# Two-head row maxima on two 64-row tiles of TensorE instead of four 32-column tiles

## The chip, the cores and the metric

The kernel runs on one core of a Trainium2 chip. The metric is device time in microseconds (us): three runs of the kernel before gave 1222.42 to 1224.43 us, median 1223.11 us. One more execution was recorded by the hardware profiler; the trace that is read below is of that one.

## The reference

Four sequences of 512 tokens, width 512, go through three blocks, each added to its input: a state-space mixer, a cross attention, and a feed-forward block with 16 experts, two per token, and a shared one. The part that the change touches is the attention:

```python
scores = jnp.einsum('bkgsd,bktd->bkgst', qh, kh) / scale   # 32 query heads, 8 key heads, depth 16
weights = jax.nn.softmax(scores, axis=-1)                  # 512 queries x 512 keys
out = jnp.einsum('bkgst,bktd->bkgsd', weights, vh)
```

Softmax needs the largest score of each query row. Any number close to it does as well, since it cancels in the quotient; it only has to keep the exponentials in range.

## The kernel before

Work in the first phase is cut into slots, numbered from -92 to 263. Every engine's program walks over the same slots in order and does in each what is due there; semaphores order the engines. A batch has 64 slots of attention (8 groups, one for each key head, of 8 units; a unit is a slot). The mixer of batch b runs in the 64 slots that begin at slot 64b - 92, two half steps a slot (`mixer_half`), and so ahead of that batch's attention. From slot 164 on no mixer is left; then the shared expert of batches 0 to 2 is computed in its place (`front`, `heavy`).

In a slot TensorE does, in this order: `scores(slot)` (keys by queries into the two banks `ps_s`, for two heads), the first half step of the mixer, `max_scores(slot + 12)` (queries by keys into the two banks `ps_m`, for two pairs of head and query block, twelve slots ahead), the second half step, and in odd slots `products` (probabilities by values). From slot 0 on every such matmul goes through `product`, which cuts it into four matmuls of 32 columns of the array each (tile positions 0, 32, 64, 96); a 32-column tile uses all 128 rows. An fp32 matmul is two instructions.

float32 queries and keys are cut into three bfloat16 parts. `q_stack` and `k_stack` hold six products of these parts stacked on 96 partitions (`Q_PART`, `K_PART`), so that one bfloat16 matmul over 96 rows gives a nearly float32 score. Three more rows of `q_stack` hold the negated maxima (in three parts) against ones in `k_stack`, which makes 99 rows for `scores`.

`ps_s` and `ps_m` are single: `scores` waits until ScalarE has taken the exponentials of the last slot's (`probabilities`, L887), `max_scores` until VectorE has reduced the last unit's (`maxima`, L680). After each group of eight units GpSimd splits the maxima (`split_max`), TensorE transposes them (`transpose_max`, L1047), ScalarE copies them, and SyncE's queue writes them into `q_stack`.

SyncE issues the DMAs in slot order: mixer weights into a ring of 10 blocks of 256 KB (`freed`, `load_w`), and the stacks (`stack_keys` in two halves, `stack_queries` in four quarters for each batch), each part row set by a DMA of its own. `prob` has six buffers. After the first phase the routed experts run, 47 tiles, one after the other.

Of the kernel before, what the change touches and what calls it, by code (L numbers as in the profile page):

```python
# [9 lines left out]
F32 = mybir.dt.float32  # L10
BF16 = mybir.dt.bfloat16
# [4 lines left out]
P = 128  # L16
# [28 lines left out]
def stream_phase(nc, dram, x1, score, ident, identb, kept, out):  # L45
# [11 lines left out]
    O_XI, O_DT, O_B = KI * P, 2 * KI * P, 2 * KI * P + H  # L57
    RING = 10
    PERIOD = 64
    G, R, DH = 8, 4, 16  # L60
    L = G - 1
    Q_PART = (0, 0, 0, 1, 1, 2)
    K_PART = (0, 1, 2, 0, 1, 0)
    KQ = len(Q_PART) * DH
    KM = KQ + 3
    UNITS = 8
    VW = 32
# [3 lines left out]
    SLOTS = B * PERIOD  # L71
    PROB = 6
    N = B * G
# [14 lines left out]
    with ExitStack() as ctx:  # L88
# [55 lines left out]
        values = sb("values", [P, TB, G, VW])  # L144
        q_stack = sb("q_stack", [KM, G * R, SEQ], BF16)
        k_stack = sb("k_stack", [KM, G, SEQ], BF16)
        mx = sb("mx", [P, G, R * TB])
# [45 lines left out]
        s_icopy, s_gate_odd = sem("inner_copied"), sem("gated_odd")  # L193
        s_ctx, s_ones, s_val = sem("context_loaded"), sem("ones_set"), sem("values_ready")
        s_ave, s_ars, s_q = sem("avar_ready"), sem("arstd_ready"), sem("q_ready")
# [52 lines left out]
        def _(sp):  # L248
# [38 lines left out]
            def stack_keys(b, h):  # L287
                if b:
                    sp.wait_ge(s_sc, PERIOD * (b - 1) + 32 * (h + 1))
                sp.wait_ge(s_prow, 16 * (5 * b + 1))  # L290
                rows = dram["part_rows"][0].rearrange("(j d) i t -> i d j t", d=DH)
                for i, p in enumerate(K_PART):
                    sp.dma_start(k_stack[i * DH:(i + 1) * DH, 4 * h:4 * h + 4, :], rows[p][:, 4 * h:4 * h + 4, :]
                                 ).then_inc(s_kst[h], 16)

            def stack_queries(b, c):
                if b:
                    sp.wait_ge(s_sc, PERIOD * (b - 1) + 16 * (c + 1))
                sp.wait_ge(s_prow, 16 * (5 * b + c + 2))
                rows = dram["part_rows"][c + 1].rearrange("(j d) i t -> i d j t", d=DH)  # L300
                for i, p in enumerate(Q_PART):
                    sp.dma_start(q_stack[i * DH:(i + 1) * DH, c * 8:(c + 1) * 8, :], rows[p]).then_inc(s_qst[c], 16)

# [101 lines left out]
        def _(pool):  # L405
# [77 lines left out]
            cut_head_weights()  # L483
            nc.gpsimd.memset(k_stack[KQ:KM, :, :], 1.0).then_inc(s_ones, 1)
            pool.wait_ge(s_ones, 1)

            for slot in span:
# [11 lines left out]
                if b < B:  # L499
# [51 lines left out]
        def _(dve):  # L551
# [123 lines left out]
            def maxima(m):  # L675
                n, u = divmod(m, UNITS)
                dve.wait_ge(s_mm, m + 1)
                if u == 0 and n >= G:
                    dve.wait_ge(s_msplit, n - G + 1)
                nc.vector.tensor_reduce(mx[:, n % G, 2 * u:2 * u + 2], ps_m[:, :, :], AX.X, ALU.max).then_inc(s_max, 1)  # L680

# [328 lines left out]
        def _(pe):  # L1010
# [151 lines left out]
            def scores(slot):  # L1162
# [6 lines left out]
                for i in range(2):  # L1169
                    r = u % 2 * 2 + i  # L1170
                    ins = product(ps_s[:, i, :], k_stack[:, g, t * P:(t + 1) * P], q_stack[:, g * R + r, :],
                                  start=True, stop=True)
                ins.then_inc(s_sc, 1)

            def max_scores(m):
                n, u = divmod(m, UNITS)
                b, g = divmod(n, G)
                if u == 0 and g % 2 == 0:
                    pe.wait_ge(s_qst[g // 2], 96 * (b + 1))
                if u == 0 and g % 4 == 0:  # L1180
                    pe.wait_ge(s_kst[g // 4], 96 * (b + 1))
                if m == 0:
                    pe.wait_ge(s_ones, 1)
                if m:
                    pe.wait_ge(s_max, m)
                for i in range(2):
# [116 lines left out]
def experts_phase(nc, dram, x1, score, ident, out, kept):  # L1303
# [26 lines left out]
    with ExitStack() as ctx:  # L1330
# [87 lines left out]
        def _(sp):  # L1418
# [37 lines left out]
            for e in range(RING, E):  # L1456

                end = sp.value_load(ends_i[0:1, e - RING:e - RING + 1], min_val=0, max_val=TILES)
                sp.wait_ge(s["dn"], end)
# [51 lines left out]
        def _(dve):  # L1511
# [83 lines left out]
            V.then(nc.vector.tensor_scalar(count[:, :], count[:, :], -P, None, ALU.bitwise_and))  # L1595
            V.then(nc.vector.tensor_copy(tiles[:, 1:1 + E], count[:, :]))
            V.then(nc.vector.tensor_tensor_scan(bounds[:, :], onesf[:, :], tiles[:, :], 0.0, ALU.mult, ALU.add))
# [286 lines left out]
def build(nc, dram, out):  # L1884
# [4 lines left out]
    with (  # L1889
# [3 lines left out]
        nc.sbuf_tensor("identb", [P, P], BF16) as identb,  # L1893
        nc.sbuf_tensor("wring", [P, 10, 512], F32) as wring,
        nc.sbuf_tensor("th", [P, 2, 512], F32) as th,
# [80 lines left out]
```

## Time and profile before

| | us |
|---|---|
| median of 3 runs | 1223.11 |
| span of the profiled execution | 1221.6 |
| around its span (median less span) | 1.5 |
| TensorE busy | 1172.0 (96%) |
| VectorE busy | 692.4 (57%) |
| ScalarE busy | 475.3 (39%) |
| GpSimd busy | 316.5 (26%) |
| mean granted TensorE clock | 0.996 |

The profiled execution's own time is its span, 1221.6 us; it lies 1.5 us below the median of the runs. A busy engine is one with an instruction under way. Matmuls overlap in the array, so that their durations add up to more than the time they take: the distance between starts says what one costs. The attention's slots 0 to 243 with `max_scores` of the column-tiled form lie between 187 and 870 us.

### The profile page before, as it was taken

What the parts mean: (1) busy time and instruction counts of PE and PEld (TensorE: products, weight loads), DVE (VectorE), ACT (ScalarE), POOL (GpSimd) and SP (SyncE); (2) the same over time, 40 slices, a digit from 0 to 9 for tenths busy, and PEclk for the clock granted to TensorE, in tenths of its full rate; (3) what the DMA queues carried; (4) which work ended last, traced back from release to release, by engine and by line L of the source; (5) the groups of instructions that cost most, each with busy time, mean ns of one, the idle gap of its engine ahead of it and who ended that gap; (6) DMA issues with size and microseconds to landing.
All of it is one profiled execution on the core that took longest, in us unless ns stands there. A gap on an engine that the chain in (4) does not pass through costs nothing. (4 is left out here: it accounts for less than half of the span.)

```text
span 1221.6 us, 31126 instructions
## 1 busy us (share of the span) xinstructions
PE 1172.0 (96%) x13185; PEld 583.6 (48%) x13186; DVE 692.4 (57%) x1146; ACT 475.3 (39%) x669; POOL 316.5 (26%) x457
## 2 busy tenths in 40 slices
PE   6999999999999999999999999999999999999996
PEld 3444434444545544545645554544444444444442
DVE  4742596756787665668675777877657222222220
ACT  3321223534554453545453455555622222222221
POOL 5112311221221230231122121111102444344443
PEclk9999999999999999999999999999999999999998
DMA  8320785104284201264500146200135666678640
GB/s 195 103 88 22 184 175 112 36 16 119 62 161 91 68 29 27 78 126 102 112 20 16 68 105 94 81 3 3 72 125 179 151 180 141 163 193 242 159 88 14
DMA packets 113057, 122.17 MB, mean 100 GB/s; under 512 B 18928, under 2 KB 78448, under 8 KB 112800
## 3 DMA queue, kind: packets, MB, share of 16 engines
q1 hardware_dynamic: 101680, 98.58, 31.6%
q0 software_dynamic: 10528, 21.12, 8.7%
q8 instruction: 99, 1.62, 0.6%
q10 hardware_dynamic: 720, 0.61, 0.2%
q14 instruction: 30, 0.25, 0.1%
HBM read 94.63 MB, written 28.97 MB: 101 GB/s over the span
## 5 line engine op out<-in xcount | busy, mean ns | idle before, releaser
L680 DVE TENSOR_REDUCE mx<-ps_m 128x2 f32<-128x1024 f32 x256 | 312.9, 1222 | 193.8 <-PE ps_m L1019 189.6
L887 ACT ACTIVATE prob<-ps_s 128x1024 f32<-128x1024 f32 x256 | 262.2, 1024 | 322.7 <-PE ps_s L1019 321.9
L1019 PE MATMUL acc<-xnT,wring 128*32 128x512 f32 x1888 | 249.6, 593 | 0.6 <-DVE first_z L616 0.6
L1836 PE MATMUL ps_gu<-ring,xgT 128*128 x376 | 176.7, 593 | 1.0 <-DVE xgT L1544 1.0
L1019 PE MATMUL ps_s<-q_stack,k_stack 99*32 99x512 bf16 x2048 | 161.9, 380 | 4.4 <-ACT prob L887 3.8
L1019 PE MATMUL ps_m<-k_stack,q_stack 96*32 96x512 bf16 x1952 | 153.5, 380 | 9.6 <-DVE mx L680 8.1
L1544 DVE COPY xgT<-ps_x 128x512 f32<-128x512 f32 x47 | 32.5, 691 | 201.4 <-PE ps_x L1806 201.4
L1204 PE MATMUL ps_o<-prob,values 128*32 128x128 f32 x4096 | 138.6, 273 | 0.0
L1204 PEld LDWEIGHTS ps_o<-prob,values 128*32 128x32 f32 x4096 | 116.5, 110 | 44.4 <-issue 38.6
L1019 PEld LDWEIGHTS ps_m<-k_stack,q_stack 96*32 96x32 bf16 x1952 | 55.9, 96 | 126.9 <-issue 71.9
L1502 POOL DMA_INDIRECT out<-y,dest x47 | 74.5, 1585 | 149.4 <-DMA out<-y,dest 135.8
L1836 PEld LDWEIGHTS ps_gu<-ring,xgT 128*128 128x128 f32 x376 | 67.7, 190 | 68.2 <-issue 68.2
L1019 PEld LDWEIGHTS ps_s<-q_stack,k_stack 99*32 99x32 bf16 x2048 | 59.2, 96 | 77.6 <-issue 41.4
L1852 PE MATMUL acc<-ring,hT 128*128 x188 | 88.6, 593 | 0.9 <-ACT hT L1694 0.9
L1017 PE MATMUL acc<-xnT,wring 128*128 128x512 f32 x184 | 85.8, 605 | 2.1 <-DVE xz L598 2.0
L1019 PEld LDWEIGHTS acc<-xnT,wring 128*32 128x32 f32 x1888 | 66.1, 109 | 43.1 <-issue 6.4
L1019 PE MATMUL acc<-wring,xz 128*32 128x512 f32 x576 | 76.5, 593 | 0.0
L598 DVE SCALAR_TENSOR_TENSOR xz<-acc,convw,xz 128x511 f32<-128x511 f32 (+2 forms) x84 | 62.6, 746 | 4.0 <-ACT xz L968 2.0
L1701 ACT ACTIVATE y<-acc,share 128x512 f32<-128x512 f32 x47 | 32.3, 687 | 83.6 <-PE acc L1852 81.9
L426 POOL TENSOR_SCALAR mneg<-mx 128x16 f32<-128x16 f32 x32 | 10.2, 318 | 195.7 <-DVE mx L680 195.7
L1017 PEld LDWEIGHTS acc<-xnT,wring 128*128 128x128 f32 x184 | 34.4, 193 | 42.1 <-issue 33.0
L1489 POOL DMA_INDIRECT xg<-xn_rows,token x47 | 47.3, 1007 | 27.7 <-DVE token L1619 13.7
(282 smaller groups left out, 1180.6 us busy)
## 6 DMA issues: line engine op xcount, KB each, us to landing
ring<-in_w_experts SPq DMA_DIRECT2D x96, 256.0 KB, 5.5
wring<-in_w_in SPq DMA_DIRECT2D x80, 256.0 KB, 4.3
q_stack<-part_rows SPq DMA_DIRECT2D x96, 128.0 KB, 4.6
wring<-in_w_out SPq DMA_DIRECT2D x32, 256.0 KB, 2.9
part_rows<-part SPq DMA_DIRECT2D x20, 384.0 KB, 3.9
out<-x SPq DMA_DIRECT2D x4, 1024.0 KB, 4.9
xt<-in_x SPq DMA_DIRECT2D x14, 256.0 KB, 4.5
k_stack<-part_rows SPq DMA_DIRECT2D x48, 64.0 KB, 3.5
```

The lines of the kernel that those rows point to most:

```text
L598: ins = nc.vector.scalar_tensor_tensor(out=xz[:, i, tap:], in0=bank(b, 5 + i)[:, :SEQ - tap], scalar=convw[:, i, 3 - tap:4 - tap], in1=xz[ ...
L680: nc.vector.tensor_reduce(mx[:, n % G, 2 * u:2 * u + 2], ps_m[:, :, :], AX.X, ALU.max).then_inc(s_max, 1)
L887: nc.scalar.activation(prob[:, slot % PROB, :, :], ps_s[:, :, :], ACT.Exp, scale=SCALE).then_inc(s_exp, 1)
L1017: return nc.tensor.matmul(dst, stationary, moving, start=start, stop=stop)
L1019: ins = nc.tensor.matmul(dst[c:c + 32, :], stationary[:, c:c + 32], moving, start=start, stop=stop, tile_position=(0, c))
L1204: ins = nc.tensor.matmul(out_rows.rearrange("p (t i) -> p t i", i=VW), values[:, t, g, :], weights[:, a, :, :], start=(t == 0 and r == 0), ...
L1489: pool.indirect_dma_start(out=xg[:, n % XG, :], out_offset=None, in_=xn_rows[:, :], in_offset=bass.IndirectOffsetOnAxis(ap=token[:, n:n + ...
L1502: pool.indirect_dma_start(out=out[:, :], out_offset=bass.IndirectOffsetOnAxis(ap=dest[:, n:n + 1], axis=0), in_=y[:, n % YB, :], in_offset ...
L1544: nc.vector.tensor_copy(xgT[:, p, :], ps_x[p][:, :]).then_inc(s["txc"], 1)
L1701: nc.scalar.activation(y[:, n % YB, :], ps_y[p][:, :], ACT.Copy, scale=share[:, n:n + 1]).then_inc(s["yc"], 1)
L1836: ins = nc.tensor.matmul(ps_gu[p][:, :], xgT[:, p, k * P:(k + 1) * P], weights(own)[:, k * 2 * F:(k + 1) * 2 * F], start=(k == 0), stop=(k ...
L1852: ins = nc.tensor.matmul(ps_y[p][:, :], hT[:, p, k * P:(k + 1) * P], weights(own)[:, WUP + k * D:WUP + (k + 1) * D], start=(k == 0), stop= ...
```

## The change

`max_scores` takes three part products (48 rows) in place of six, for each of its two results. The stack is laid out in seven sections of 16 partitions, so that three leading products stand at partitions 0 to 47 for even heads and at 64 to 111 for odd ones. The two results are the same query block of an even and an odd head. Each is one matmul on a tile of 64 rows and all 128 columns, at row 0 or row 64. `scores` takes 115 rows in place of 99, with two versions of the keys (even and odd). So `k_stack` is twice as large, and the weight ring goes from 10 blocks to 8 and `prob` from 6 buffers to 5. GpSimd fills sections that nothing is loaded to; SyncE issues 8 DMAs for a quarter of the queries and 12 for a half of the keys, in place of 6 and 6. In the last phase a count of tiles is held at one at least.

```diff
-    RING = 10
+    RING = 8
-    Q_PART = (0, 0, 0, 1, 1, 2)
-    K_PART = (0, 1, 2, 0, 1, 0)
-    KQ = len(Q_PART) * DH
+    EVEN_Q, EVEN_K = (0, 0, 1, 2, 0, 1, None), (0, 1, 0, 0, 2, 1, None)
+    ODD_Q, ODD_K = (0, 2, 1, None, 0, 1, 0), (2, 0, 1, None, 0, 0, 1)
+    KQ = len(EVEN_Q) * DH
     KM = KQ + 3
+    LEADING = 3 * DH
+    HALF_ROWS = P // 2
-    PROB = 6
+    PROB = 5
-        q_stack = sb("q_stack", [KM, G * R, SEQ], BF16)
-        k_stack = sb("k_stack", [KM, G, SEQ], BF16)
+        q_stack = sb("q_stack", [P, G * R, SEQ], BF16)
+        k_stack = sb("k_stack", [P, 2, G, SEQ], BF16)
...
-                for i, p in enumerate(K_PART):
-                    sp.dma_start(k_stack[i * DH:(i + 1) * DH, 4 * h:4 * h + 4, :], rows[p][:, 4 * h:4 * h + 4, :]
-                                 ).then_inc(s_kst[h], 16)
+                for odd, parts in enumerate((EVEN_K, ODD_K)):
+                    for i, p in enumerate(parts):
+                        if p is not None:
+                            sp.dma_start(k_stack[i * DH:(i + 1) * DH, odd, 4 * h:4 * h + 4, :],
+                                         rows[p][:, 4 * h:4 * h + 4, :]).then_inc(s_kst[h], 16)
...
+                for i, (even, odd) in enumerate(zip(EVEN_Q, ODD_Q)):
+                    dst = q_stack[i * DH:(i + 1) * DH, c * 8:(c + 1) * 8, :]
+                    if even == odd:
+                        sp.dma_start(dst, rows[even]).then_inc(s_qst[c], 16)
+                        continue
+                    for at, p in enumerate((even, odd)):
+                        if p is not None:
+                            sp.dma_start(dst[:, at::2, :], rows[p][:, at::2, :]).then_inc(s_qst[c], 16)
...
-            nc.gpsimd.memset(k_stack[KQ:KM, :, :], 1.0).then_inc(s_ones, 1)
+            nc.gpsimd.memset(k_stack[96:P, :, :, :], 1.0).then_inc(s_ones, 1)
...
+                    if m == 14 and b == 0:
+                        pool.wait_ge(s_val, G)
+                        nc.gpsimd.memset(k_stack[32:64, 1, :, :], 0.0).then_inc(s_ones, 1)
+                        pool.wait_ge(s_ones, 2)
+                    if m == 16 and b == 0:
+                        nc.gpsimd.memset(q_stack[96:P, 0::2, :], 0.0).then_inc(s_blank, 1)
+                        pool.wait_ge(s_blank, 1)
+                    if m == 18 and b == 0:
+                        nc.gpsimd.memset(q_stack[32:64, 1::2, :], 0.0).then_inc(s_blank, 1)
+                        pool.wait_ge(s_blank, 2)
...
-                    ins = product(ps_s[:, i, :], k_stack[:, g, t * P:(t + 1) * P], q_stack[:, g * R + r, :],
-                                  start=True, stop=True)
+                    ins = product(ps_s[:, i, :], k_stack[0:KM, i, g, t * P:(t + 1) * P],
+                                  q_stack[0:KM, g * R + r, :], start=True, stop=True)
...
+                pair, t = divmod(u, TB)
                 for i in range(2):
-                    r, t = u // 2, 2 * (u % 2) + i
-                    ins = product(ps_m[:, i, :], q_stack[0:KQ, g * R + r, t * P:(t + 1) * P], k_stack[0:KQ, g, :],
-                                  start=True, stop=True)
+                    rows = slice(HALF_ROWS * i, HALF_ROWS * i + LEADING)
+                    ins = nc.tensor.matmul(ps_m[:, i, :], q_stack[rows, g * R + 2 * pair + i, t * P:(t + 1) * P],
+                                           k_stack[rows, i, g, :], start=True, stop=True,
+                                           tile_position=(HALF_ROWS * i, 0))
```

## Rows read from the trace of the kernel before

**Rows 1.** Busy time by stretch, from start to end in us (x instructions).

```profile
156.00:187.00 31.00, 28.84 (x84) 10.88 (x86) 29.02 (x36) 8.26 (x14) 3.66 (x7) 1.00 0.77 160
187.00:690.00 503.00, 493.62 (x7984) 258.25 (x7980) 340.95 (x427) 234.62 (x291) 106.31 (x201) 1.00 0.32 72
690.00:870.00 180.00, 173.44 (x3146) 85.82 (x3138) 142.60 (x209) 100.43 (x115) 32.14 (x79) 1.00 0.28 68
```

**Rows 2.** Timeline of TensorE in the mixer's slots: start, length.

```profile
368.03 1.04 PE L1019 MATMUL acc<-xnT,wring 128*32 128x512 f32 x8
368.89 0.62 PE L1019 MATMUL ps_m<-k_stack,q_stack 96*32 96x512 bf16 x8
369.33 1.04 PE L1019 MATMUL acc<-xnT,wring 128*32 128x512 f32 x8
```

**Rows 3.** Timeline of TensorE, 694 to 696 us: full-width transposes between column tiles.

```profile
694.75 0.62 PE L1019 MATMUL ps_m<-k_stack,q_stack 96*32 96x512 bf16 x8 [0.35 <-DVE mx L680]
695.30 0.66 PE L1220 MATMUL acc<-ident,xt 128*128 128x128 f32 x4
695.88 0.61 PE L1019 MATMUL ps_s<-q_stack,k_stack 99*32 99x512 bf16 x8
```

**Rows 4.** Timeline of TensorE, 312 to 314 us: the same with lagging tiles.

```profile
312.40 0.68 PE L1019 MATMUL ps_s<-q_stack,k_stack 99*32 99x512 bf16 x8
313.00 0.66 PE L1040 MATMUL ps_t<-ident,xz 128*128 128x128 f32 x4
```

**Rows 5.** The transposes of L1040: ns min/median/max.

```profile
L1040 PE MATMUL ps_t<-ident,xz x64: 272/273/330, 134.6 to 738.6; 128*128 128x128 f32 x64
```

**Rows 6.** Instructions that write `ps_m`: ns min/median/max.

```profile
L1019 PEld LDWEIGHTS ps_m<-k_stack,q_stack x1952: 92/96/101, 188.6 to 869.0; 96*32 96x32 bf16 x196
...
L1017 PEld LDWEIGHTS ps_m<-k_stack,q_stack x24: 95/98/100, 156.1 to 185.5; 96*128 96x128 bf16 x24
L1017 PE MATMUL ps_m<-k_stack,q_stack x24: 377/380/390, 156.5 to 185.7; 96*128 96x512 bf16 x24
```

**Rows 7.** Waits, 690 to 870 us: us in total, times, longest.

```profile
DVE mx L680 <- PE ps_m L1019: 34.0, 47, 1.6
PEld ps_m L1019 <- DVE mx L680: 30.3, 51, 1.5
```

**Rows 8.** Timeline of TensorE without the mixer, 758 to 761 us.

```profile
758.01 0.61 PE L1019 MATMUL ps_m<-k_stack,q_stack 96*32 96x512 bf16 x8
758.45 1.03 PE L1019 MATMUL acc<-wring,th 128*32 128x512 f32 x8
759.32 0.60 PE L1019 MATMUL ps_s<-q_stack,k_stack 99*32 99x512 bf16 x8
759.96 0.61 PE L1019 MATMUL ps_m<-k_stack,q_stack 96*32 96x512 bf16 x8
```

**Rows 9.** Timeline of VectorE and ScalarE, same slots.

```profile
758.68 1.23 DVE L680 TENSOR_REDUCE mx<-ps_m 128x2 f32<-128x1024 f32 x1 [0.72 <-PE ps_m L1019]
760.63 1.23 DVE L680 TENSOR_REDUCE mx<-ps_m 128x2 f32<-128x1024 f32 x1 [0.72 <-PE ps_m L1019]
...
759.97 1.02 ACT L887 ACTIVATE prob<-ps_s 128x1024 f32<-128x1024 f32 x1 [0.91 <-PE ps_s L1019]
```

**Rows 10.** Timeline of TensorE between two batches' mixers, 302 us.

```profile
302.30 0.61 PE L1019 MATMUL ps_m<-k_stack,q_stack 96*32 96x512 bf16 x8 [0.89 <-DVE mx L680]
```

**Rows 11.** Timeline of GpSimd at the start.

```profile
23.31 3.51 POOL L484 MEMSET k_stack<- 3x4096 bf16 x1
...
79.69 2.49 POOL L524 TENSOR_TENSOR bsb<-gains,bsb 128x512 f32<-128x512 f32 x2 [42.71 <-DMA gains<-gain_rows]
```

**Rows 12.** Timeline of SyncE's issues (SPq) before the second batch.

```profile
121.87 3.56 SPq L261 DMA_DIRECT2D wring<-in_w_in  x4
125.47 2.96 SPq L293 DMA_DIRECT2D k_stack<-part_rows  x6
```

**Rows 13.** Timeline of TensorE there: the second batch's first weight block.

```profile
129.23 1.98 PE L1017 MATMUL acc<-xnT,wring 128*128 128x512 f32 x4
```

More of the change, by code:

```diff
@@ L61, in stream_phase @@
     L = G - 1
-    Q_PART = (0, 0, 0, 1, 1, 2)
-    K_PART = (0, 1, 2, 0, 1, 0)
-    KQ = len(Q_PART) * DH
+    EVEN_Q, EVEN_K = (0, 0, 1, 2, 0, 1, None), (0, 1, 0, 0, 2, 1, None)
+    ODD_Q, ODD_K = (0, 2, 1, None, 0, 1, 0), (2, 0, 1, None, 0, 0, 1)
+    KQ = len(EVEN_Q) * DH
     KM = KQ + 3
+    LEADING = 3 * DH
+    HALF_ROWS = P // 2
+    Q_LOADS = sum(1 if a == o else (a is not None) + (o is not None) for a, o in zip(EVEN_Q, ODD_Q))
+    K_LOADS = sum(a is not None for a in EVEN_K + ODD_K)
     UNITS = 8
@@ L193, in stream_phase @@
         s_icopy, s_gate_odd = sem("inner_copied"), sem("gated_odd")
-        s_ctx, s_ones, s_val = sem("context_loaded"), sem("ones_set"), sem("values_ready")
+        s_ctx, s_ones, s_val = sem("context_loaded"), sem("key_rows_set"), sem("values_ready")
+        s_blank = sem("query_rows_blank")
         s_ave, s_ars, s_q = sem("avar_ready"), sem("arstd_ready"), sem("q_ready")
@@ L289, in stack_keys @@
                     sp.wait_ge(s_sc, PERIOD * (b - 1) + 32 * (h + 1))
+                else:
+                    sp.wait_ge(s_ones, 2)
                 sp.wait_ge(s_prow, 16 * (5 * b + 1))
                 rows = dram["part_rows"][0].rearrange("(j d) i t -> i d j t", d=DH)
-                for i, p in enumerate(K_PART):
-                    sp.dma_start(k_stack[i * DH:(i + 1) * DH, 4 * h:4 * h + 4, :], rows[p][:, 4 * h:4 * h + 4, :]
-                                 ).then_inc(s_kst[h], 16)
+                for odd, parts in enumerate((EVEN_K, ODD_K)):
[3 more added lines that the diff above has]
+                                         rows[p][:, 4 * h:4 * h + 4, :]).then_inc(s_kst[h], 16)
             def stack_queries(b, c):
@@ L298, in stack_queries @@
                     sp.wait_ge(s_sc, PERIOD * (b - 1) + 16 * (c + 1))
+                else:
+                    sp.wait_ge(s_blank, 2)
                 sp.wait_ge(s_prow, 16 * (5 * b + c + 2))
                 rows = dram["part_rows"][c + 1].rearrange("(j d) i t -> i d j t", d=DH)
-                for i, p in enumerate(Q_PART):
-                    sp.dma_start(q_stack[i * DH:(i + 1) * DH, c * 8:(c + 1) * 8, :], rows[p]).then_inc(s_qst[c], 16)
+                for i, (even, odd) in enumerate(zip(EVEN_Q, ODD_Q)):
[6 more added lines that the diff above has]
+                            sp.dma_start(dst[:, at::2, :], rows[p][:, at::2, :]).then_inc(s_qst[c], 16)
             def max_rows(n):
@@ L679, in maxima @@
                     dve.wait_ge(s_msplit, n - G + 1)
-                nc.vector.tensor_reduce(mx[:, n % G, 2 * u:2 * u + 2], ps_m[:, :, :], AX.X, ALU.max).then_inc(s_max, 1)
+                pair, t = divmod(u, TB)
+                columns = mx[:, n % G, :].rearrange("p (r t) -> p r t", t=TB)
+                nc.vector.tensor_reduce(columns[:, 2 * pair:2 * pair + 2, t], ps_m[:, :, :], AX.X, ALU.max
+                                        ).then_inc(s_max, 1)
             def front(a, r):
@@ L1178, in max_scores @@
                 if u == 0 and g % 2 == 0:
-                    pe.wait_ge(s_qst[g // 2], 96 * (b + 1))
+                    pe.wait_ge(s_qst[g // 2], 16 * Q_LOADS * (b + 1))
                 if u == 0 and g % 4 == 0:
-                    pe.wait_ge(s_kst[g // 4], 96 * (b + 1))
-                if m == 0:
-                    pe.wait_ge(s_ones, 1)
+                    pe.wait_ge(s_kst[g // 4], 16 * K_LOADS * (b + 1))
                 if m:
                     pe.wait_ge(s_max, m)
+                pair, t = divmod(u, TB)
                 for i in range(2):
-                    r, t = u // 2, 2 * (u % 2) + i
-                    ins = product(ps_m[:, i, :], q_stack[0:KQ, g * R + r, t * P:(t + 1) * P], k_stack[0:KQ, g, :],
-                                  start=True, stop=True)
+                    rows = slice(HALF_ROWS * i, HALF_ROWS * i + LEADING)
+                    ins = nc.tensor.matmul(ps_m[:, i, :], q_stack[rows, g * R + 2 * pair + i, t * P:(t + 1) * P],
+                                           k_stack[rows, i, g, :], start=True, stop=True,
+                                           tile_position=(HALF_ROWS * i, 0))
                 ins.then_inc(s_mm, 1)
@@ L1456, in _ @@
             for e in range(RING, E):
-                end = sp.value_load(ends_i[0:1, e - RING:e - RING + 1], min_val=0, max_val=TILES)
+                end = sp.value_load(ends_i[0:1, e - RING:e - RING + 1], min_val=1, max_val=TILES)
                 sp.wait_ge(s["dn"], end)
@@ L1595, in _ @@
             V.then(nc.vector.tensor_scalar(count[:, :], count[:, :], -P, None, ALU.bitwise_and))
-            V.then(nc.vector.tensor_copy(tiles[:, 1:1 + E], count[:, :]))
+            V.then(nc.vector.tensor_scalar(tiles[:, 1:1 + E], count[:, :], float(P), None, ALU.max))
             V.then(nc.vector.tensor_tensor_scan(bounds[:, :], onesf[:, :], tiles[:, :], 0.0, ALU.mult, ALU.add))
@@ L1893, in build @@
         nc.sbuf_tensor("identb", [P, P], BF16) as identb,
-        nc.sbuf_tensor("wring", [P, 10, 512], F32) as wring,
+        nc.sbuf_tensor("wring", [P, 8, 512], F32) as wring,
         nc.sbuf_tensor("th", [P, 2, 512], F32) as th,
```

## The prediction

> **What bounds the kernel now.** I read the busy times by stretch first. From 187 to 690 us TensorE has a matmul under way 493.6 of 503 us, at full granted clock (1.00, the 2.4 GHz level); VectorE is busy 341 us [rows 1]. These are slots 0 to about 163, with a mixer half step on either side of `max_scores`: 3.1 us a slot. Whatever TensorE does more or less in such a slot, the end moves by. From 690 to 870 us (about 80 slots, 2.2 us each) the waits say something else: the weight loads for `ps_m` wait 51 times for VectorE's reduction, and the reduction 47 times for `ps_m` [rows 7]. Each stops for the other, since `ps_m` is single. The timeline shows the loop: `ps_m` starts at 758.01, the reduction at 758.68, it takes 1.23, and the next `ps_m` starts at 759.96, 1.95 us after the last [rows 8, 9]. So two stages with two bounds: TensorE's work in one, a loop of latencies in the other.
>
> **TensorE's price of the maxima, in the mixer's slots.** Eight column-tile matmuls cost the distance to the next group: 369.33 - 368.89 = 0.44 us, as two rounds of about 0.22 us, four tiles at a time [rows 2]. One row of full width gives the same streaming time in another form: a full-width matmul of the same size lasts 380 ns [rows 6], one tile matmul too; a result over 128 columns is one stream of 0.22 us. Two of them at once on different rows would thus save 0.22 us.
>
> But the array is used in another shape, between two uses in the old one. No row of before has a 64-row tile. The nearest are full-width transposes between column tiles. `ps_m` to transposes takes 0.55 us instead of 0.44: 0.11 to go in. The first of them lasts 330 ns where the others last 273 [rows 5]: 0.06 for its fp32 weight load of 128 columns, which nothing covers. From the first start to the last are 0.66 - 0.27 = 0.39 us, less the 0.06 and by three: 0.11 each. Four should take 0.44; they take 0.58 until the column tiles run again [rows 3]. Of these 0.14, 0.06 is that load, and the rest, 0.085, is the way back out, to which 0.02 comes for the uncovered fp32 loads behind it. Where one of the four column tiles lags the others (length 0.68, not 0.61), going in costs 0.17 instead [rows 4]; such lags come once in eight slots, behind `transpose_max`, so 0.01 a slot on average.
>
> The Trainium skill (TensorEngine Tiling (Array Packing), Tiling Modes) says that changing the tiling mode, not just the tile, drains TensorE. The trace agrees, with the 0.11 and 0.09 us above, and by that rule, priced so, half of what the second round gives is lost at each end; without it the change would take 0.2 us off each such slot.
>
> The sum for a mixer slot: before 0.44. After: 0.11 in, 0.01 for the uncovered bfloat16 load, 0.01 until the second matmul starts (eight of 0.38 take 0.62 in two rounds 0.22 apart, which leaves 0.02 for four starts [rows 2, 6]), 0.215 for the streams at the same time, 0.085 out, 0.02 behind it, 0.01 for lags: 0.46. That is +0.025 us a slot. I take the load at 0.01 because the two loads of before, 32 and 128 columns wide, last 96 and 98 ns, the same [rows 6]; if it is as dear as the transposes' (0.06, and the second's not under the first) the slot has +0.12. If going in and out cost nothing, the slot has -0.20. If the two matmuls follow each other, +0.24. The bounds of this term are these, -0.20 and +0.24, the inner ones, with half a drain and with exposed loads, -0.07 and +0.12.
>
> The skill's TensorE: Matmul & The Clock Gate (LDWEIGHTS) puts a load at its columns by 1.2 GHz, an estimate of 107 ns for 128 columns against 27 for 32; two such loads uncovered would, by that estimate, put +0.2 us on a slot where the sum above has +0.025. The 98 and 96 ns above don't bear it out for bfloat16 in full width; no row shows it for a 64-row tile.
>
> 157 slots of this kind (163, less 6 between the mixers of two batches, where the 0.89 us wait shows the loop of the late slots [rows 10]): +3.9 us.
>
> **The late slots.** In the loop, the reduction starts 0.67 us after `ps_m` because it waits for the second round. With both matmuls in one round this is 0.21 us less: 0.46 + 1.23 + 0.05 = 1.74. The way in is mostly free: `ps_s` began 0.64 us before `ps_m`, and it streams for 0.44 [rows 8], so 0.2 us of idle array lie there. What is late next? TensorE's own path: from `ps_m` 758.45 - 758.01 = 0.44 (now 0.35 with the way out), 0.87 for a half step, 0.44 for `ps_s`, and 0.11 in: 1.77. And ScalarE's loop: `ps_s` to exponential 0.65 (759.97 - 759.32), 1.02, 0.05 back to TensorE as for the reduction: 1.72 [rows 8, 9]. So such an interval goes from 1.95 to about 1.77: 0.18 less. Stepping through VectorE's timeline, 50 late slots are of this kind ([rows 7] count 51). In 26 of them VectorE is idle for 0.18 or more ahead of the reduction (0.72 like the rows shown), which give 4.7 us; in the other 24 it has other work until 0.10 to 0.15 before it (some 12 of them), or right up to it; they give 1.6 us together. Sum 6.3. The other 30 late slots are bound by TensorE's work and get 30 x 0.025 = +0.75. The 6 slots between batches give 6 x 0.15 = 0.9. In slots -12 to -1 both TensorE (28.8) and VectorE (29.0 of 31 us) are full [rows 1]; the reductions follow VectorE's other work within 0.1 us there: 0.3 us less over the stretch, at most.
>
> **Parts at nothing.** GpSimd's first memset has 8192 elements a partition for 4096 at 3.51 us [rows 11]: 3.5 us more. It delays the step-size chain and VectorE's residual work. The cover is TensorE's projections, 3.44 us of matmuls for each 128 channels (4 x 2 x 0.43), four banks deep, so that a bank's reader may be late by a block; without that cover it costs 3.5 us. The three new memsets (3.5, 7 and 7 us by the same rate) fall into GpSimd's idle time of 42.7 us before 79.69 [rows 11]. SyncE: an issue takes 0.5 us (2.96 for 6 [rows 12]), so a half of the keys blocks the queue 3 us longer, a quarter of the queries 1 us. Queued behind are mixer weights, which with 8 blocks are still asked for some 14 slots ahead, and the maxima rows, 4 slots later than the stacks' issue. Same bytes of queries, 128 KB x 6; keys twice 384 KB a half, small beside the 0.3 of DMA time used. The tight place is the batch border: the next batch's first block can be asked for only when the output weights are used up, 121.87 [rows 12], lands some 4.5 us later and is wanted at 129.23 [rows 13], 2.5 us to spare. Five buffers of `prob`: the one that slot s writes was read at the end of slot s - 2 at the latest, ahead of `scores(s)` on TensorE itself, so no wait. 115 rows for 99 stream in the same time, as 96 and 99 do. The held count adds no instruction.
>
> **Sum.** +3.9 + 0.75 - 6.3 - 0.9 - 0.3 = -2.85 us on the execution of 1221.6 us: 1218.75. The runs' median lies 1.5 above: 1220.3 us, 0.23% faster. Even stands at +0.04 us a slot (7.5 us of gain over 187 slots), so the sign hangs on 15 ns a slot.
>
> **Rivals.**
> Exposed loads (slower): the weights of a 64-row tile, 128 columns, can't be put in before the old shape has drained, and both loads lie open as the transposes' first does. For: 0.06 us in the rows of the transposes. Against: 96 and 98 ns. +0.12 x 187 = +22.4, the loop gains 0.1 less (-3.5): +19, 1242 us. It decides from 0.04 us a slot on.
> One after the other (slower): the second matmul waits for the first. +0.24 x 187 = +45, no gain in the loop: 1268 us. No row speaks for it; column tiles do run together.
> The loop does not shorten (slower by little): the reduction starts no earlier, or ScalarE's loop, at 1.72 with no lag, holds it. +3.9 + 0.75 - 1.2: 1226.6 us.
> Half a drain (faster): a 64-row tile empties sooner than 128 rows. -0.07 x 187 = -13, -7.5 in the loops: 1203 us.
> No drain (faster): -0.20 x 187 - 8.5: 1177 us. Against: the 0.11 and 0.09 us.
> Late weights or queue: 2.5 us to spare at the batch borders are lost and more; +2 on the sum: 1222 us, no change.
>
> **Chances.** The sum as worked out 0.38 (with its terms uncertain by some 3 us, 0.24 faster, 0.12 same, 0.02 slower); no drain 0.08; half a drain 0.10; exposed loads 0.14; one after the other 0.10; loop not shorter 0.12 (0.03 of it same); late weights 0.08 (0.06 same, 0.02 slower). Within 0.2%, 2.4 us, is what a measurement of this kernel can't tell from no change. Faster 0.42, same 0.21, slower 0.37. The range leaves out no drain and one after the other, 0.18: 1203 to 1242 us. The likeliest case alone spans 1216 to 1224.
>
> **What would show it.** Right: `ps_m` as two matmuls within 10 ns, 0.31 to 0.33 us to the next group in mixer slots, 0.11 us longer before them; 0.46 us from `ps_m` to the reduction; intervals near 1.77 where they were 1.95; 187 to 690 us longer by 3 us, 690 to 870 shorter by 6. Wrong: starts 0.2 us apart, or a distance from `ps_m` to the next group over 0.4, or one under 0.25; waits of TensorE for weight blocks after a batch border.

## The result and the profile after

The changed kernel takes 1234.57 us, the median of 9 runs (1233.38 to 1240.77), beside 1223.11 for 9 runs of the kernel before (1221.58 to 1231.04). The ratio is 1.0081, 95% interval 1.0057 to 1.0106: 0.8% slower, where the forecast was 0.23% faster. The time lies inside the range and on the other side of no change.

The profiled execution of the changed kernel has a span of 1232.7 us, 11.1 more than before. I compared the two traces between the same instructions of both: the scores' first matmul in slots 0, 164, 244 and 255.

| us | before | after | difference |
|---|---|---|---|
| start to slot 0 | 186.9 | 200.1 | +13.2 |
| slot 0 to 164, mixers running | 506.9 | 507.8 | +0.8 |
| slot 164 to 244, late slots | 177.2 | 169.2 | -8.0 |
| slot 244 to 255 | 21.0 | 21.0 | 0.0 |
| slot 255 to the end | 329.6 | 334.6 | +5.1 |

Differences are taken before rounding. In the attention slots the change gave 7.2 us. It lost 13.2 ahead of the first slot, where the prediction had put it at nothing.

**The slots.** TensorE's timeline in a mixer slot of after, which answers to [rows 2]:

```profile
396.27 1.04 PE L1049 MATMUL acc<-xnT,wring 128*32 128x512 f32 x8
397.25 0.39 PE L1217 MATMUL ps_m<-k_stack,q_stack 48*128 48x512 bf16 x2
397.57 1.07 PE L1049 MATMUL acc<-xnT,wring 128*32 128x512 f32 x8
```

The two matmuls of a slot start 3 ns apart in the trace, so they stream together. From `acc` to `ps_m` are 0.98 us (before 0.86), from `ps_m` to the next group 0.32 (before 0.44). Going in costs 0.12, and 0.12 is got back: no gain, no loss. The medians over 92 slots of each trace agree: 0.86 and 0.43 before, 0.98 and 0.32 after. The instructions themselves, answering to [rows 6]:

```profile
L1217 PEld LDWEIGHTS ps_m<-k_stack,q_stack x512: 92/92/102, 170.4 to 875.3; 48*128 48x128 bf16 x171
L1217 PE MATMUL ps_m<-k_stack,q_stack x512: 372/387/606, 170.4 to 875.3; 48*128 48x512 bf16 x171
```

The weight load of 128 columns takes 92 ns in the median, where that of 32 took 96. TensorE and VectorE in the late slots, answering to [rows 8, 9]:

```profile
770.16 0.39 PE L1217 MATMUL ps_m<-k_stack,q_stack 48*128 48x512 bf16 x2
770.48 1.06 PE L1049 MATMUL acc<-wring,th 128*32 128x512 f32 x8
771.36 0.62 PE L1049 MATMUL ps_s<-q_stack,k_stack 115*32 115x512 bf16 x8
771.91 0.39 PE L1217 MATMUL ps_m<-k_stack,q_stack 48*128 48x512 bf16 x2
```

```profile
770.59 1.23 DVE L709 TENSOR_REDUCE mx<-ps_m 128x2 f32<-128x1024 f32 x1 [0.61 <-PE ps_m L1217]
772.34 1.23 DVE L709 TENSOR_REDUCE mx<-ps_m 128x2 f32<-128x1024 f32 x1 [0.53 <-PE ps_m L1217]
```

The reduction starts 0.43 us after `ps_m` instead of 0.67, and the interval is 1.75 us instead of 1.95. Slot by slot, 50 of the 80 late slots are shorter, by 0.20 us on average and 9.9 together; the other 30 are longer by 0.01 each, but for one of 1.5 at the beginning (slot 165). The waits from 703 to 877 us, answering to [rows 7] (us in total, times, longest), still show both engines stopping for each other:

```profile
PEld ps_m L1217 <- DVE mx L709: 28.9, 56, 1.7
DVE mx L709 <- PE ps_m L1217: 28.4, 42, 1.6
```

**The start.** VectorE's timeline in after:

```profile
23.30 6.75 DVE L592 TENSOR_SCALAR var_eps<-mv 128x4 f32<-128x4 f32 x1
...
40.33 0.55 DVE L606 TENSOR_SCALAR xt<-xt,mv,rstd 128x512 f32<-128x512 f32 x1
40.79 3.82 DVE L604 TENSOR_SCALAR x<-xt,keep 128x512 f32<-128x512 f32 x1
44.53 7.22 DVE L606 TENSOR_SCALAR xt<-xt,mv,rstd 128x512 f32<-128x512 f32 x1
51.67 2.30 DVE L625 SCALAR_TENSOR_TENSOR xz<-acc,convw,xz 128x511 f32<-128x511 f32 x3
```

GpSimd's beside it, answering to [rows 11]:

```profile
23.11 6.92 POOL L501 MEMSET k_stack<- 32x8192 bf16 x1
...
40.58 3.75 POOL L537 MEMSET k_stack<- 32x4096 bf16 x1
44.38 7.09 POOL L540 MEMSET q_stack<- 32x8192 bf16 x1
51.53 7.08 POOL L543 MEMSET q_stack<- 32x8192 bf16 x1
```

Read them side by side. The eight TENSOR_SCALARs that write the normalized input (`xt`) and its residual (`x`) are alike, and the first six take 0.55 us each. The seventh starts 0.21 us after the first zero fill and lasts until 44.61, 0.28 us behind the fill's end. The eighth starts 0.15 us after the next fill and lasts until 51.75, again until just behind it. The first row is the plainest: four elements a partition, 6.75 us, because it started during the fill of ones. VectorE is held until GpSimd's instruction is through. The other direction shows too, and is small: each zero fill starts 0.2 to 0.3 us before a TENSOR_SCALAR ends and takes 3.75, 7.09 and 7.08 us, where the same fills take 3.50 and 6.92 when none is under way (first experiment below). The convolution (SCALAR_TENSOR_TENSOR, reading PSUM) starts at 51.67 us, 13.04 later than before (38.63), and runs beside the third fill in its usual 2.30.

TensorE's timeline shows who waits for that:

```profile
42.11 3.60 PE L1047 MATMUL acc<-xnT,wring 128*128 128x512 f32 x8
54.03 6.51 PE L1047 MATMUL acc<-xnT,wring 128*128 128x512 f32 x8 [8.32 <-DVE xz L625]
...
162.26 1.09 PE L1070 MATMUL ps_t<-ident,xz 128*128 128x128 f32 x4 [2.26 <-DVE rest L700]
163.13 7.37 PE L1047 MATMUL acc<-xnT,wring 128*128 128x512 f32 x14
```

The projections run out of PSUM banks and stand for 8.32 us. The next eight matmuls then take 6.51 us where eight took 3.60. The granted clock fell during the pause: it is 1.00 from 46 to 48 us and 0.50, the lower level (1.2 GHz), from 50 to 59; from 0 to 60 us it is 0.91 on average, 1.00 before. The second batch's first step-size projection comes at 138.8 us, 10.6 later than before; the wait and the slower matmuls together are 11.2. The last two rows are a second, smaller loss: between that projection and the first `ps_m` lie 31.6 us, 28.3 before.

The sign of this was in the trace of before, in a row of VectorE that I had not put beside [rows 11]:

```profile
25.50 1.34 DVE L565 TENSOR_SCALAR var_eps<-mv 128x4 f32<-128x4 f32 x1
```

It starts during the old memset (23.31, 3.51 us), takes 1.34 us where the same shape took 0.18 at 34.55, and ends with it, at 26.84.

### The profile page after: what moved, and what is told of

It is laid out like the page before. It is cut to its first block and busy times, and to the rows that moved or that the text cites. A ratio compares the mean times of both kernels' runs of the same rounds, so it can differ in the third digit from the quotient of the medians.

```text
span 1232.7 us, 28285 instructions
## 1 busy us (share of the span) xinstructions
PE 1171.1 (95%) x11720; PEld 517.8 (42%) x11722; DVE 707.3 (57%) x1146; ACT 474.7 (39%) x669; POOL 338.8 (27%) x460
## 5 line engine op out<-in xcount | busy, mean ns | idle before, releaser
L1049 PE MATMUL ps_s<-q_stack,k_stack 115*32 115x512 bf16 x2048 | 159.7, 380 | 4.9 <-ACT prob L917 4.9
L1574 DVE COPY xgT<-ps_x 128x512 f32<-128x512 f32 x47 | 32.5, 692 | 205.1 <-PE ps_x L1836 186.2
L1532 POOL DMA_INDIRECT out<-y,dest x47 | 74.5, 1585 | 154.3 <-DMA out<-y,dest 101.9
L1217 PE MATMUL ps_m<-k_stack,q_stack 48*128 48x512 bf16 x512 | 100.0, 387 | 8.1 <-DVE mx L709 7.8
L1047 PE MATMUL acc<-xnT,wring 128*128 128x512 f32 x184 | 90.5, 632 | 9.6 <-DVE xz L625 9.6
L1217 PEld LDWEIGHTS ps_m<-k_stack,q_stack 48*128 48x128 bf16 x512 | 24.6, 92 | 178.6 <-issue 133.2
L1049 PEld LDWEIGHTS ps_s<-q_stack,k_stack 115*32 115x32 bf16 x2048 | 54.5, 97 | 80.3 <-issue 42.8
L1049 PEld LDWEIGHTS acc<-xnT,wring 128*32 128x32 f32 x1888 | 48.3, 108 | 52.0 <-issue 34.8
L443 POOL TENSOR_SCALAR mneg<-mx 128x16 f32<-128x16 f32 x32 | 10.2, 318 | 186.5 <-DVE mx L709 186.2
L1047 PEld LDWEIGHTS acc<-xnT,wring 128*128 128x128 f32 x184 | 34.8, 201 | 52.6 <-issue 37.7
```

Source lines behind the costliest of these rows:

```text
L1047: return nc.tensor.matmul(dst, stationary, moving, start=start, stop=stop)
L1049: ins = nc.tensor.matmul(dst[c:c + 32, :], stationary[:, c:c + 32], moving, start=start, stop=stop, tile_position=(0, c))
L1217: ins = nc.tensor.matmul(ps_m[:, i, :], q_stack[rows, g * R + 2 * pair + i, t * P:(t + 1) * P], k_stack[rows, i, g, :], start=True, stop=True,
L1532: pool.indirect_dma_start(out=out[:, :], out_offset=bass.IndirectOffsetOnAxis(ap=dest[:, n:n + 1], axis=0), in_=y[:, n % YB, :], in_offset ...
L1574: nc.vector.tensor_copy(xgT[:, p, :], ps_x[p][:, :]).then_inc(s["txc"], 1)
```

## The experiments

The tables below give slot 0 and the end in us of each one's profiled execution; before has 186.9 and 1221.6, after 200.1 and 1232.7. A ratio is to the kernel before on the same chip. Theories at the beginning: the fills on GpSimd hold VectorE (A); the keys' and queries' transfers in SyncE's queue are what delays the start (B).

Times of the start come from one trace each and vary. In the seven traces in which none of the eight large TENSOR_SCALARs is held and nothing is put ahead of them, the second batch's first step-size projection lies between 124.9 and 128.3 us; one program, run twice, has 125.6 and 128.2, and the kernel before, at 128.2, is among the late ones. So a difference of the start alone is good to some 3 us.

**Fills behind the residual.** The zero fills wait until VectorE's eight TENSOR_SCALARs are through.

```diff
                     if m == 14 and b == 0:
+                        pool.wait_ge(s_ln, 2 * TB)
                         pool.wait_ge(s_val, G)
                         nc.gpsimd.memset(k_stack[32:64, 1, :, :], 0.0).then_inc(s_ones, 1)
```

> The changed kernel, with one wait added: GpSimd's three later fills of the stacks start only when VectorE has finished the residual and normalised rows of the second batch. Theory A (VectorE is shut out while a GpSimd memset runs: TENSOR_SCALAR from SBUF to SBUF took 3.8 and 7.2 us beside the fills, 0.55 otherwise): VectorE's convolutions start some 10 us earlier (51.7 to about 42 us), TensorE's wait of 8.3 us goes, attention begins near 190 us and not 200, total 1234.6 - 10 = about 1224 us. Rival B (the start is late because the issue queue and the smaller weight ring hold TensorE): attention still begins near 200 us, total within 2 us of 1234.6.

Measured: 1217.56 us (6 runs, 1216.24 to 1224.93), ratio 0.9948 (0.9912 to 0.9985). Slot 0 at 187.9, end 1215.2. All of the fills are still there, GpSimd first and VectorE below:

```profile
42.04 3.50 POOL L538 MEMSET k_stack<- 32x4096 bf16 x1 [1.33 <-DVE xt L607]
45.60 6.92 POOL L541 MEMSET q_stack<- 32x8192 bf16 x1
```

```profile
41.44 0.54 DVE L607 TENSOR_SCALAR xt<-xt,mv,rstd 128x512 f32<-128x512 f32 x1
41.89 2.31 DVE L626 SCALAR_TENSOR_TENSOR xz<-acc,convw,xz 128x511 f32<-128x511 f32 x3
44.12 2.30 DVE L626 SCALAR_TENSOR_TENSOR xz<-ps_s,convw,xz 128x511 f32<-128x511 f32 x3
46.34 0.68 DVE L637 SCALAR_TENSOR_TENSOR xz<-th,xz 128x512 f32<-128x512 f32 x1
```

Nothing is held by these fills any more: beside them VectorE runs SCALAR_TENSOR_TENSORs, from PSUM in 2.31 us and from two inputs in SBUF in 0.68, both as before. One wait of GpSimd turns a loss of 0.8% into a gain of 0.5%. The start came as A had it (slot 0 12.2 us earlier than in after); the total fell 6 us more than expected, and of the 17.6 us between the two traces 4.3 lie in the last phase, which this edit doesn't touch. The fill of ones, still in its place, delays the convolution by 3.26 us (41.89 against 38.63), yet the second batch's projection is at 128.3 us (before 128.2), and TensorE waits for no convolution ahead of it: those 3.3 us were covered.

**The fills alone, on the kernel before.** Three memsets of the same sizes at the same places, and batch 0's keys and queries wait for them; the attention is untouched.

```diff
+                    if m == 14 and b == 0:
+                        pool.wait_ge(s_val, G)
+                        nc.gpsimd.memset(k_stack[32:64, :, :], 0.0).then_inc(s_blank, 1)
+                        pool.wait_ge(s_blank, 1)
+                    if m == 16 and b == 0:
+                        nc.gpsimd.memset(q_stack[64:96, 0::2, :], 0.0).then_inc(s_blank, 1)
+                        pool.wait_ge(s_blank, 2)
...
+                        nc.gpsimd.memset(q_stack[32:64, 1::2, :], 0.0).then_inc(s_blank, 1)
```

> The kernel before, with three fills of GpSimd at the places and of the sizes of the changed kernel (4096, 8192, 8192 bfloat16 elements a partition, on partitions that are loaded later); the first fill stays at 4096. Theory A: VectorE's TENSOR_SCALAR is held for about 4 and 7 us, attention begins 7 to 10 us later (186.9 to about 195), total about 1231 to 1233 us. Rival B: nothing moves, 1223 us.

Measured: 1245.25 us (4 runs, 1242.09 to 1246.70), ratio 1.0143 (1.0099 to 1.0188). Slot 0 at 201.4. VectorE:

```profile
37.13 3.81 DVE L594 TENSOR_SCALAR xt<-xt,mv,rstd 128x512 f32<-128x512 f32 x1
40.86 7.22 DVE L592 TENSOR_SCALAR x<-xt,keep 128x512 f32<-128x512 f32 x1
48.00 7.22 DVE L594 TENSOR_SCALAR xt<-xt,mv,rstd 128x512 f32<-128x512 f32 x1
```

Here three are held, one by each fill, and slot 0 comes 14.6 us later with no other part of the change. That is more than the 7 to 10 expected, which counted two. A stands.

**The changed kernel again.** No edit.

> The changed kernel itself again, for a second trace. If the last phase (from the last scores to the end) is longer in it by its own doing, it shows 333 to 336 us again, for 329.5 in the kernel before; if that was the luck of one execution, it comes out between 329 and 338 without order.

Measured: 1241.83 us (2 runs, 1241.66 and 1241.99), ratio 1.0126 (1.0075 to 1.0176). Slot 0 at 208.8, end 1240.2. It is the same program as after, and its trace has three TENSOR_SCALARs held where after's has two:

```profile
40.26 3.81 DVE L606 TENSOR_SCALAR xt<-xt,mv,rstd 128x512 f32<-128x512 f32 x1
43.99 7.22 DVE L604 TENSOR_SCALAR x<-xt,keep 128x512 f32<-128x512 f32 x1
51.14 7.22 DVE L606 TENSOR_SCALAR xt<-xt,mv,rstd 128x512 f32<-128x512 f32 x1
58.28 2.30 DVE L625 SCALAR_TENSOR_TENSOR xz<-acc,convw,xz 128x511 f32<-128x511 f32 x3
```

TensorE's wait for VectorE's convolution is 16.7 us instead of 8.3. How many of the eight get through before the first fill, and so whether one is left for the third, is a matter of a few hundred ns: the fill starts 2.10 us after the first of the eight here, 2.53 in after. After's nine runs lie in two groups, six at 1233.4 to 1236.2 and three at 1239.8 to 1240.8 us. It is tempting to read these as two held and three held, but that isn't shown: the kernel before, where none is held, has such groups as well (seven runs to 1224.5 us, two at 1230.2 and 1231.0), and so has fills late below (four at 1217.1 to 1217.8, four from 1224.5 up).

**All fills late, and keys later.** Also the fill of ones goes behind the residual; in the second of these kernels, the keys' second step moves from slot -32 to -24. It was run twice.

```diff
-            nc.gpsimd.memset(k_stack[96:P, :, :, :], 1.0).then_inc(s_ones, 1)
-            pool.wait_ge(s_ones, 1)
...
                     if m == 14 and b == 0:
+                        pool.wait_ge(s_ln, 2 * TB)
                         pool.wait_ge(s_val, G)
+                        nc.gpsimd.memset(k_stack[96:P, :, :, :], 1.0).then_inc(s_ones, 1)
+                        pool.wait_ge(s_ones, 1)
```

```diff
-KHALF_AT = (-32, 1)
+KHALF_AT = (-24, 1)
```

Fills alone:

> The changed kernel with all four fills behind the second batch's residual, the key stacks issued where the change has them. It parts the two causes of the late start that the version with later keys took away together. If the 12 key DMAs ahead of the rows of x cost TensorE 2.2 us and a stretch at the half clock, the way from the second batch's first projection to the first maxima takes about 30 us here (28.4 with later keys, 28.3 in the kernel before); if they cost nothing, 28.4 us. Attention begins near 185.5 us against 183.6.

Both:

> The changed kernel with all four fills behind the residual of the second batch, and the first half of the key stacks issued 8 slots later, behind the next batch's rows of x. If both causes of the late start are right (fills 11 us, and the 12 key DMAs that delay x, VectorE's statistics and a transpose by 2.3 us with a stretch at half clock behind it), attention begins at 186 to 187 us and the total is 1234.6 - 13.5 = 1221 us, or below by what the last phase's scatter gives. If only the fills count, it begins near 190 us and the total is about 1224 us.

> The version with late fills and later keys again, in more rounds, to have its ratio to the kernel before with a narrower interval: its trace was 1211.2 us long for 1221.6, 10 us less, of which 3 in the start, 7 in the late slots and none in the last phase. If the runs agree, the ratio is 0.991 to 0.996 and the interval stays below 1.

| | median us (runs, extremes) | ratio (interval) | projection to first `ps_m` | slot 0 | end |
|---|---|---|---|---|---|
| fills late | 1221.16 (8, 1217.08 to 1228.02) | 0.9973 (0.9943 to 1.0004) | 30.1 | 187.9 | 1223.5 |
| and keys later | 1218.74 (10, 1213.07 to 1226.57) | 0.9946 (0.9916 to 0.9976) | 28.4 | 183.6 | 1211.2 |
| the same again | 1221.52 (12, 1213.63 to 1223.51) | 0.9956 (0.9932 to 0.9980) | 28.4 | 186.2 | 1220.8 |

The fourth column is the piece from the second batch's first step-size projection to the first `ps_m`: 28.3 before, 31.6 after. This is where B has its share. SyncE's issues in after, against [rows 12] with 2.96 us for six of the keys:

```profile
136.12 6.00 SPq L302 DMA_DIRECT2D k_stack<-part_rows  x12
142.16 2.58 SPq L266 DMA_DIRECT2D wring<-in_w_in  x4
144.79 2.04 SPq L256 DMA_DIRECT2D xt<-in_x  x4
```

Behind the twelve issues stands not only the weight block that I had looked at, but the next input rows (`xt`). They come late, so do VectorE's statistics and `rest`, and a transpose of TensorE waits. The waits of TensorE for `rest` with fills late, then with keys later too:

```profile
PE ps_t L1072 <- DVE rest L702: 2.3, 1, 2.3
```

```profile
PE ps_t L1072 <- DVE rest L702: 0.6, 1, 0.6
```

0.6 is also the value of before; with the wait gone the whole piece is 28.4 us again. So B is right for 1.8 us (30.1 to 28.4) in the kernels with the fills late. After is longer by another 1.5 us, and the traces show where. Behind a wait of the same length stand, in fills late:

```profile
151.64 0.63 PE L1072 MATMUL ps_t<-ident,xz 128*128 128x128 f32 x4 [2.34 <-DVE rest L702]
152.10 6.23 PE L1049 MATMUL acc<-xnT,wring 128*128 128x512 f32 x14
```

In after the same transposes and 14 matmuls take 1.09 and 7.37 us (rows above), 1.55 us more from first start to last end. The granted clock is 0.53 from 162 to 164 us and 0.62 from 164 to 166 there, and 1.00 throughout in fills late. It falls like that behind this wait in the three traces with TENSOR_SCALARs held and twelve issues (after, its repeat, the tiles of 32 columns below) and not in fills late or behind the residual; why, no run shows. The totals don't resolve B's share: the intervals of the three rows overlap, and two executions of one program end 9.6 us apart.

**The other shape of tile.** In after, each 64-row matmul is cut into four of 32 columns.

```diff
-                    ins = nc.tensor.matmul(ps_m[:, i, :], q_stack[rows, g * R + 2 * pair + i, t * P:(t + 1) * P],
...
-                                           tile_position=(HALF_ROWS * i, 0))
+                    for c in range(0, P, 32):
+                        ins = nc.tensor.matmul(ps_m[c:c + 32, i, :],
+                                               q_stack[rows, g * R + 2 * pair + i, t * P + c:t * P + c + 32],
+                                               k_stack[rows, i, g, :], start=True, stop=True,
+                                               tile_position=(HALF_ROWS * i, c))
```

> The changed kernel with each of the two 64-row matmuls cut into four column tiles of 32 (eight matmuls of 64 rows by 32 columns). If the price of a change of shape lies in the columns (128 against 32), the way in and out costs nothing and a mixer slot falls by 0.2 us against the changed kernel: 187 to 690 us shorter by about 30 us, total about 1200 us. If any change of tile shape, rows too, is paid, the slot stays at 0.43 to 0.44 us for the maxima and the total within 3 us of 1234.6.

Measured: 1241.21 us (4 runs, 1236.32 to 1248.63), ratio 1.0104 (1.0058 to 1.0150). Its trace has three TENSOR_SCALARs held, so the total is to be read beside the 1241.83 of the changed kernel again. Slot 0 to 164 takes 510.8 us, 3.0 more than after.

```profile
388.22 1.04 PE L1049 MATMUL acc<-xnT,wring 128*32 128x512 f32 x8
389.20 0.41 PE L1218 MATMUL ps_m<-k_stack,q_stack 48*32 48x512 bf16 x8
389.54 1.06 PE L1049 MATMUL acc<-xnT,wring 128*32 128x512 f32 x8
```

In 0.98 and out 0.34, to after's 0.98 and 0.32. The columns are those of the neighbours now, only the rows differ, and the 0.12 us on the way in stay. A change of rows alone is paid as well.

**Full width, one after the other.** In before, each head's maxima as one matmul over 96 rows and 128 columns, in the usual mode.

```diff
-                    ins = product(ps_m[:, i, :], q_stack[0:KQ, g * R + r, t * P:(t + 1) * P], k_stack[0:KQ, g, :],
-                                  start=True, stop=True)
+                    ins = nc.tensor.matmul(ps_m[:, i, :], q_stack[0:KQ, g * R + r, t * P:(t + 1) * P],
+                                           k_stack[0:KQ, g, :], start=True, stop=True)
```

> The kernel before, with the maxima's matmuls uncut: two matmuls of 96 rows by all 128 columns, one after the other, between column tiles. It has the change of shape without two matmuls at a time. Theory (a change of tile shape costs 0.11 us in and 0.09 to 0.10 out, and the changed kernel pays that with the 0.215 us of the round it saves): the maxima cost 0.64 us a mixer slot, 187 to 690 us longer by 157 x 0.2 = 31 us, late slots a few us longer, total 1223 + 35 = 1258 us. Rival (the price is that of changing the rows of a tile, not its columns): no more than 1226 us.

Measured: 1262.82 us (4 runs, 1261.80 to 1267.20), ratio 1.0308 (1.0264 to 1.0353); slot 0 to 164 in 541.8 us, +34.8, 0.21 a slot.

```profile
386.28 1.04 PE L1019 MATMUL acc<-xnT,wring 128*32 128x512 f32 x8
387.26 0.60 PE L1188 MATMUL ps_m<-k_stack,q_stack 96*128 96x512 bf16 x2
387.79 1.06 PE L1019 MATMUL acc<-xnT,wring 128*32 128x512 f32 x8
```

The same 0.98 in, and 0.53 out: two streams after each other instead of one. This separates what the change does: going in and out costs about the same in both kernels, and running both heads at once saves 0.21 us, which just pays for it.

**Only the rings.** In before, the weight ring and `prob` cut as the change cuts them.

```diff
-    RING = 10
-    PROB = 6
+    RING = 8
+    PROB = 5
```

> The kernel before with 8 blocks in the weight ring for 10 and 5 buffers of prob for 6. Theory: nothing waits for either, within 2 us of the kernel before, no wait of TensorE for a weight block. Rival: at the batch borders, where a block is asked for 7 us ahead of its use, TensorE waits, 2 us or more a batch.

Measured: 1224.36 us (8 runs, 1222.18 to 1233.15), ratio 0.9992 (0.9958 to 1.0027). Nothing, as forecast.

**A later start alone.** The last phase took 5.1 us longer in after. I suspected that it depends on when it begins. In before, two memsets of 6.92 us each ahead of the first deviations push all later work back.

```diff
+            steps.then(nc.gpsimd.memset(q_stack[64:96, 0::2, :], 0.0))
+            steps.then(nc.gpsimd.memset(q_stack[64:96, 0::2, :], 0.0))
             deviations(0)
```

> The kernel before, with two fills of 7 us at the very start of GpSimd's program, so that all that follows is shifted by some 10 to 14 us and nothing else changes. In the traces so far the last phase is the longer the later it starts (881 and 885 us: 330.6 and 330.3; 892: 329.5; 898: 334.6; 906: 337.8; 908: 338.4). If it is the time since the start that counts, it takes 335 us or more here and the total is 1223 + 12 + 6 = 1241 us; if the length hangs on something in those kernels, or on luck, it stays near 330 us and the total is near 1235 us.

Measured: 1236.58 us (10 runs, 1231.19 to 1241.26), ratio 1.0075 (1.0047 to 1.0103). Slot 0 is 8.0 us later, slot 255 7.8, and the last phase takes 336.1 us instead of 329.6. That seemed to bear the idea out. The later kernels, and this table over all profiled executions, took it back:

| us | slot 255 | last phase |
|---|---|---|
| keys later | 880.6 | 330.6 |
| keys later again | 884.3 | 336.5 |
| fills behind residual | 884.9 | 330.3 |
| fills late | 885.9 | 337.6 |
| small rings | 889.1 | 332.0 |
| before | 892.0 | 329.6 |
| after | 898.1 | 334.6 |
| before shifted | 899.8 | 336.1 |
| before with fills | 906.4 | 337.8 |
| changed again | 906.9 | 333.3 |
| tiles of 32 columns | 908.3 | 338.5 |
| full width | 927.4 | 332.8 |

The same program has 330.6 and 336.5, and the latest start has 332.8. In before the phase is paced by GpSimd's indirect transfers: the wait for the previous one is 135.8 us over 44 of 47. In after that wait is 101.9 us over 32, and in 14 cases ScalarE's result (`y`) came last, 47.1 us. The phase's length varies by up to 9 us between executions, and no run here ties that to the start or to the change.

## Why the prediction was wrong, step by step

**The failed step is "Parts at nothing".** It said: "The three new memsets (3.5, 7 and 7 us by the same rate) fall into GpSimd's idle time of 42.7 us". They do, and their durations were right (3.75, 7.09, 7.08). What was missing is the other engine. I asked who waits for GpSimd and not who can't run beside it. Here VectorE's TENSOR_SCALARs from SBUF to SBUF are held for the whole of a fill, and the kernel has eight of them just where the fills stand. With the first fill it cost 10.6 us up to the second batch when two were held (after), and 19.3 when three were (the changed kernel again, 147.5 against 128.2; 16.3 with tiles of 32 columns), each good to some 3 us. Moving the fills by one wait took it to 0.1; putting them alone into before brought it to 14.6. This is shown from both sides.

The Trainium skill has this rule (SBUF — State Buffer, Who interferes with whom): VectorE in a two-port mode and GpSimd share a pair of ports under an exclusive lock, whoever issues first has it for the whole instruction, and a VectorE instruction with two SBUF inputs only meets a GpSimd instruction that reads SBUF. The traces agree: TENSOR_SCALAR at 7.22 us for 0.55, SCALAR_TENSOR_TENSOR with two SBUF inputs at 0.68 beside a memset, which writes only, and 2.31 from PSUM. Beside a GpSimd instruction that reads SBUF one with two SBUF inputs is held: in before shifted a SCALAR_TENSOR_TENSOR of 128x4 starts at 31.10, 0.03 us after a CAST on GpSimd, and takes 1.03 us like it, against 0.16 in before. In which mode the TENSOR_SCALARs run no row says; that they are held is what the rows show. By the durations of [rows 11], a rival could have been worked out: each fill holds one TENSOR_SCALAR, some 17 us of VectorE in the stretch where it feeds TensorE's banks. None of my rivals was that one.

**The first fill, "3.5 us more", covered.** Right with the other fills out of the way: 3.3 us later on VectorE, and no wait of TensorE for it. In after the cover was too short for both: the convolution came 13.0 us later and TensorE stood for 8.3, so some 3 of these 8.3 are, by an estimate from the two numbers, the first fill's.

**SyncE's queue.** Half right. Twice the issues of keys took 6.00 us, 3.0 more, as worked out. But I named the weight block as the tight one behind them, with 2.5 us to spare; no wait for a weight block shows. What is late next are the input rows and all that hangs on them: statistics, `rest`, a transpose, the projections behind it. The runs put 1.8 us on the keys' issues, and in after the clock fell behind that wait, 1.5 more.

**TensorE's price, +0.025 us a mixer slot.** The mechanism was right in every part, the size off by 0.02. In 0.12 (forecast 0.11); matmuls 3 ns apart, no exposed loads, so neither that rival nor "one after the other" came. The distance behind `ps_m` is 0.32 (forecast 0.31 to 0.33). Stretch by stretch +0.8 us, where 163 slots as forecast give 3.0 after the border slots. The forecast's own terms add up to 0.46 for 0.44, which is 0.02 a slot and not 0.025; that would be 3.1 us in place of 3.9. The terms for uncovered reloads and lags, 0.02 and 0.01, are about what is too much; the runs don't separate them. The bounds of the sequential case were good too: +34.8 us in 164 slots for full width, where +0.24 a slot without the loop would be 39.

**The late slots, -6.3 + 0.75.** The mechanism was right, the size too small: -8.0 for -5.55. The interval is 1.75 us, forecast 1.77. But all 50 slots of the kind lost about 0.20 us, where the forecast gave 24 of them a third of that, and the slots bound by TensorE paid 0.01 and not 0.025.

**The last phase.** No term; +5.1 in the profiled execution. Open, as above. The sum of the differences is 13.2 + 0.8 - 8.0 + 5.1 = 11.1 us; the medians differ by 11.5.

**What is gained when the fills are out of the way.** Four sets of runs have them out of the way. Fills behind the residual (0.9948) and keys later, twice (0.9946 and 0.9956), have intervals that end below 1; fills late alone (0.9973) has one that ends just above it. That is 3 to 7 us faster than before. In all four traces the attention slots give 7.2 to 8.2 us, all of it in the late slots; the start and the last phase vary by as much from one execution to the next. The change as the prediction meant it was forecast at -2.85 us, and fills behind the residual, which moves nothing else, has some -6.

## What to carry to other kernels

An instruction put into an engine's idle time is free only if no other engine is shut out by it: beside its place, write down what VectorE runs during each new GpSimd instruction, and look in the trace of before for a small instruction that lasts as long as its neighbour on the other engine. Order such work behind the sensitive stretch with a wait, not by luck. And follow a queue behind a longer issue to every transfer in it, not only to the one that looks tightest.

## What was unexpected of the hardware

A VectorE instruction of four elements a partition took 6.75 us, because a fill had begun 0.19 us earlier. The same program had two instructions held in one execution and three in another, with 200.1 and 208.8 us to slot 0. Going in from 128-row column tiles costs 0.12 us for each of the three other shapes tried, for 64 rows with the columns unchanged as much as for full width; a bfloat16 weight load of 128 columns on a 64-row tile takes 92 ns and shows no price of its own. A pause of 8.3 us cost more than itself: the clock fell during it, and the eight matmuls behind it ran 2.9 us longer. A pause of 2.3 us was followed by a stretch at the lower clock in after and by none in fills late. And a last phase whose code doesn't change took from 329.6 to 338.5 us.
